# Last attention: the first quarter of each turn's output projection is put ahead of the last weighted sum

## The reference

```python
q = (hidden_states @ Wq).reshape(B, Sq, H, D)
k = (encoder_hidden_states @ Wk).reshape(B, Skv, H, D)
v = (encoder_hidden_states @ Wv).reshape(B, Skv, H, D)
q = rmsnorm(q, gq)
k = rmsnorm(k, gk)
scores = jnp.einsum('bqhd,bkhd->bhqk', q, k) * scale
attn = jax.nn.softmax(scores, axis=-1)
out = jnp.einsum('bhqk,bkhd->bqhd', attn, v)
out = out.reshape(B, Sq, H * D)
return out @ Wo
...
x = x + _L3_xattn_ref(_layernorm(x, axis=-1), ctx_1024, ...)
x = x + _L3_ffn_ref(_layernorm(x, axis=-1), ...)
```

## Time and profile before

| | us |
|---|---|
| median of 3 runs | 1499.85 |
| lowest and highest run | 1498.85, 1501.99 |
| profiled execution, its own time | 1488.37 |
| span of the profiled execution | 1486.6 |

### The profile page before, as it was taken

How to read it: one execution, slowest core, us unless ns; L and a number is a source line. 1 busy time by engine, 2 the same in 40 slices (tenths; PEclk the granted TensorE clock), 3 DMA queues, 4 the chain that set the end, 5 groups by cost and what they waited for, 6 DMA issues and landing times.

```text
span 1486.6 us, 20851 instructions
## 1 busy us (share of the span) xinstructions
PE 1303.5 (88%) x6620; PEld 906.9 (61%) x6620; DVE 1048.2 (71%) x2211; ACT 720.4 (48%) x1836; POOL 216.2 (15%) x227
## 2 busy tenths in 40 slices
PE   8688869986998668999998689985999999889998
PEld 4344445552333244677676589974888888764555
DVE  7999987888896787777877623225666666668565
ACT  5788823443775665555544112223666666633111
POOL 0132220000000002222220173111111111201000
PEclk9899979995999869999999799997999999989999
DMA  5122240015330200000004198845222222101230
GB/s 189 71 99 99 86 191 1 1 28 87 65 59 6 78 1 1 1 37 1 36 1 134 43 345 309 301 176 180 94 71 71 71 71 71 35 1 47 77 91 29
DMA packets 77776, 124.61 MB, mean 84 GB/s; under 512 B 44965, under 2 KB 56430, under 8 KB 72352
## 3 DMA queue, kind: packets, MB, share of 16 engines
q1 hardware_dynamic: 75824, 119.37, 24.8%
q0 software_dynamic: 1872, 4.22, 0.7%
HBM read 88.28 MB, written 26.24 MB: 77 GB/s over the span
## 4 chain that ended last, share of the span: by engine, by line
PE 66%; DVE 18%; issue 7%; ACT 4%; DMA 3%; POOL 1%; SPq 1%; DVEq 1%; ACTq 0%; POOLq 0%
DVE roomA L753 5%; PE psum L3181 5%; PE psum L2397 5%; PE psum L1978 4%; PE psum L2687 4%; PE psum L2739 4%; PE psum L873 4%; PE psum L2717 4%; PE psum L2020 3%; PE psum L2765 3%; PE psum L3191 3%; PE psum L2408 2%; PE psum L2010 2%; PE psum L1374 2%; DVE roomB L1535 2%
## 5 line engine op out<-in xcount | busy, mean ns | idle before, releaser
L2804 ACT ACTIVATE roomA<-psum,roomA 128x256 f32<-128x256 f32 x128 | 70.9, 559 | 92.7 <-DVE roomA L2870 92.4
L2066 ACT ACTIVATE roomA<-psum,roomA 128x128 f32<-128x128 f32 (+1 forms) x128 | 53.2, 426 | 88.4 <-DVE roomA L2141 88.2
L1535 DVE TENSOR_REDUCE roomB<-psum 128x2 f32<-128x512 f32 x128 | 82.1, 686 | 10.8 <-PE psum L1374 9.3
L2539 DVE SCALAR_TENSOR_TENSOR roomA<-roomA,psum 128x512 f32<-128x512 f32 x23 | 15.9, 690 | 101.7 <-ACT roomA L2444 101.7
L1978 PE MATMUL psum<-own,roomB 128*128 128x512 f32 x160 | 75.0, 594 | 3.4 <-DVE roomA L2133 2.1
L1941 POOL TENSOR_TENSOR roomA<-roomA 128x512 f32<-128x512 f32 x40 | 51.0, 1275 | 176.8 <-DVE roomA L2134 176.8
L3181 PE MATMUL psum<-roomA,roomB 128*112 128x512 f32 (+1 forms) x168 | 74.8, 593 | 0.3 <-DVE roomA L3409 0.3
L2739 PE MATMUL psum<-roomA 128*128 128x256 f32 x256 | 68.3, 389 | 6.0 <-DVE roomA L2882 4.4
L753 DVE TENSOR_TENSOR_SCAN roomA<-roomA 128x1024 f32<-128x1024 f32 x32 | 73.1, 2284 | 0.0
L1374 PE MATMUL psum<-roomB,roomA 48*128 48x256 bf16 x256 | 53.0, 308 | 16.2 <-DVE roomB L1535 8.7
L2717 PE MATMUL psum<-roomA 128*128 128x256 f32 x256 | 65.6, 379 | 1.7 <-ACT roomA L2804 1.7
(11 more groups left out here) (526 smaller groups left out, 3328.0 us busy)
## 6 DMA issues: line engine op xcount, KB each, us to landing
roomB<-m_w_dram SPq DMA_DIRECT2D x12, 1536.0 KB
roomA<-m_w_dram SPq DMA_DIRECT2D x11, 1536.0 KB
a_kv_ready<-roomB SPq DMA_DIRECT2D x32, 512.0 KB, 3.1
roomA<-a_kv_ready SPq DMA_DIRECT2D x8, 1024.0 KB, 4.8
roomA<-a_kv_ready SPq DMA_DIRECT2D x16, 512.0 KB, 4.3
roomB<-a_w_dram SPq DMA_DIRECT2D x4, 1280.0 KB, 5.9
roomB<-f_w_dram SPq DMA_DIRECT2D x8, 624.0 KB, 3.9
roomA<-f_c_rows SPq DMA_DIRECT2D x6, 512.0 KB, 3.9
```

The lines of the kernel that those rows point to most:

```text
L1535: dve.tensor_reduce(maxneg[:, hp // 8, :, m, hp % 8], g.bank(m).rearrange("p (q k) -> p q k", k=S), AX.X, ALU.max, negate=True).then_inc(s ...
```

## The change

The loop over the four quarters becomes a function, `project_out(k)`. Quarter 0, with the wait for Wo, is put into slot 10, ahead of `weigh(7)`. Quarters 1 to 3 stay behind the slots. Each quarter k now waits for `a4_ot` at t * 8 + 5 + k, which is the copy of its own unit 4 + k; before, quarters 0 to 2 all waited for unit 6's and quarter 3 for unit 7's. Quarters 0 and 1 wait for `a4_exp` at t * 8 + 7 and t * 8 + 8; before, both waited for t * 8 + 8. The matmuls, the banks and the other waits are the same, and no other engine's program is changed.

```diff
+            def project_out(k):
+                pe.wait_ge(s["a4_ot"], t * 8 + 5 + k)
+                if k < 2:
+                    pe.wait_ge(s["a4_exp"], t * 8 + 7 + k)
+                elif jobs:
+                    pe.wait_ge(*((s["a4_kt"], t * 4 + 8) if k == 2 else (s["a4_qt"], t * 4 + 7)))
+                for r in range(2):
+                    i = 2 * k + r
+                    for q in range(2):
+                        ins = pe.matmul(g.bank(OB[k])[:, r * D:(r + 1) * D], OT[:, q, i * P:(i + 1) * P], w_o[:, q, :],
+                                        start=(q == 0), stop=(q == 1))
+                ins.then_inc(s["a4_out"], 1)
+
             for slot in range(SLOTS):
...
                 if units and 2 <= slot < 10:
                     turn_weights(slot - 2)
+                if units and slot == SLOTS - 1:
+                    pe.wait_ge(s["a4_wo"], t * 16 + 16)
+                    project_out(0)
                 if units and 3 <= slot < 11:
                     weigh(slot - 3)
             if units:
-                pe.wait_ge(s["a4_wo"], t * 16 + 16)
-                for k in range(4):
-                    pe.wait_ge(s["a4_ot"], t * 8 + (8 if k == 3 else 7))
-                    if k < 2:
-                        pe.wait_ge(s["a4_exp"], t * 8 + 8)
-                    elif jobs:
-                        pe.wait_ge(*((s["a4_kt"], t * 4 + 8) if k == 2 else (s["a4_qt"], t * 4 + 7)))
-                    for r in range(2):
-                        i = 2 * k + r
-                        for q in range(2):
-                            ins = pe.matmul(g.bank(OB[k])[:, r * D:(r + 1) * D], OT[:, q, i * P:(i + 1) * P], w_o[:, q, :],
-                                            start=(q == 0), stop=(q == 1))
-                    ins.then_inc(s["a4_out"], 1)
+                for k in range(1, 4):
+                    project_out(k)
```

## The result

| us | before | changed |
|---|---|---|
| median of 4 runs each | 1499.35 | 1486.16 |
| lowest and highest of them | 1496.17, 1501.99 | 1483.71, 1487.62 |
| profiled execution, its own time | 1488.37 | 1487.62 |
| span of the profiled execution | 1486.6 | 1485.9 |

The ratio is 0.9925, with a 95% interval from 0.9899 to 0.9951: 7 to 15 us faster. The forecast was 1493.7, with a range from 1491.0 to 1497.3. The two profiled executions differ by only 0.7 us, so neither the gain nor its surplus can be read off the spans.

A forecast was written before the change was run, and what follows sets the result against it. PE was taken to bound the kernel, busy 35.48 of a 36.10 us turn. Savings of 5.5 us (turns 0 to 6) and 0.6 (turn 7), 6.1 together, took 1499.85 to 1493.7, range 1491.0 to 1497.3.

The forecast's parts named there:

- The stop and its price: End of turns 0 to 6, PE's stop ahead of weigh(7): 0.52 us idle plus 0.27 restart, 0.79 per turn.
- Nothing takes the stop's place: End of turns 0 to 6: four quarters and weigh(7) run as one stream without stops; 7 x 0.79 = 5.5 us.
- Turn 7: Last turn, without jobs: add(1) comes earlier, set by DVE rather than PE, handing 0.60 us to the next block.
- The sum: Whole attention: 5.5 us from turns 0 to 6 plus 0.6 from turn 7, 6.1 us.
- The first two rivals: Time given back within the next turn: 1499.3, chance 0.07; early quarter 0 itself stops PE: 1499.9, chance 0.03.
- the base from which the sum was taken off: Whole kernel: 6.1 us taken unscaled off the runs' median of 1499.85, giving 1493.7.
- The third rival, the clock: Behind the attention, earlier arrival meets PE's clock change elsewhere: loss of 3 us or more, chance 0.08; slower kernel 0.03.

The follow-up runs named there:

- two halves of the change: Kernel before with only the new order (quarter 0 ahead of weigh(7), old waits): 1.0009; with only the new waits in the old order: 1.0006.

## Why the prediction was right, and where it failed

- *The stop and its price.* Right. 0.79 us per turn, seven times, were forecast; the turn went from 36.10 to 35.33 and the tail from 9.44 to 8.66.
- *Nothing takes the stop's place.* Right, each queue as worked out but for one reading: the V load behind weigh(7) is not issued 0.1 us later but 0.95, counted from weigh(6) (1211.36 before; 1214.68 in a turn that runs 2.37 us later now). It costs nothing, since no new stop follows.
- *Turn 7.* Right in mechanism. The term was mis-sized: 0.83 instead of 0.60, since DVE's add begins before the copy ahead of it has ended (1317.06 against 1317.14), and likewise the second add behind the statistics.
- *The sum.* 6.3 us measured in the attention against 6.1, in the pair of traces in which no clock falls there.
- *The first two rivals.* Both out: the turn is shorter, and quarter 0 never waits.
- *The step that failed: the base from which the sum was taken off, and the range around it.* "I take it off unscaled: 1493.7" used a median of 3 runs, and the range's bounds came from the 3 us by which those three differed. The 151 runs of the kernel before on all chips (one of 7281 us left out) have a mean of 1495.0 and go from 1488.1 to 1505.4; the 22 of the changed kernel have a mean of 1487.7. The first four of the one averaged 4.2 us above that and the first four of the other 1.7 below. That is 5.9 us of the first difference, and no term of the forecast had to do with it. Whether it was luck alone isn't shown: in the later timings no four successive runs of the kernel before average over 1499.0, while those first four have 1499.2. Over all runs the gain is 7.4 us, give or take 1.4 (two standard errors): 0.9951. Without that first measurement it is 6.9, give or take 1.5. So the 6.1 us were about right, and the 13.2 of the first measurement are not the size of the gain.
- *The third rival, the clock.* Right in kind, but too narrow. "PE's clock is at its upper level, 2.4 GHz, through the attention" was read from one trace, and a fall inside the attention was put at nothing. Five traces have the end stop, POOL's fills in their old place and no added matmuls: the kernel before three times and its two halves of the change. In four of them the clock fell in turn 6, at a cost of 3.0 us from the end of the 1.85 us stop on, and the one at hand for the prediction was the fifth. It fell in none of three traces of the changed kernel. Behind the attention the loss that the rival spoke of did come in two of three traces of the changed kernel, 3.5 and 1.7 us against the first one. By the six traces the two nearly cancel, 2.0 us won and 1.9 lost, and 6.4 us remain, within the error of the 7.4. How often each comes in unprofiled runs was not measured.

## What to carry to other kernels

Between two operations that share one buffer, put independent work that lasts until the buffer is free again, and no more. Here weigh(7) began 0.68 us after it could have (1209.36 to 1210.04, turn 4 before): half a quarter of 0.87 us was enough, and two quarters delayed the adds of turn 7. Such a move gains only together with waits that name the very unit it needs; either half alone gave 1.001. Where gains of half a per cent matter, take the base from more than three runs; take several traces of the kernel before, too, and look at the granted clock in each, because a shift by 2 us upstream can add or remove 3 us in a place that the edit does not touch.

## What the runs showed of the hardware

- Fills by POOL of 128x4096 and 32x1024 float32 words, one behind the other, held DVE's 128x256 TENSOR_SCALAR pair for 4.32 us instead of 0.62; the pair ends 0.15 us behind the second fill. With the fills beside an output projection that cost was gone (the turn's tail, the copies and the adds in it as long as without).
- One stop of PE of 1.85 us tips the clock from 2.4 to 1.2 GHz or does not, by when it comes: a delay of 1.73 us in front of the attention flipped the outcome in both kernels, and one of 3.46 us flipped it back, in one trace each. Counted from the end of the low stretch ahead, 0.25 us were enough to tell the first two traces of one kernel apart (256.35 us, no fall; 256.60 us, fall).
- A fall cost 3.0 us in the five traces with an end stop of 0.52 or 0.59 us behind it, and 1.7 us in the one without.
- DVE started an add 0.08 us before its preceding copy had ended in the records.
